# A fused cross-attention and feed-forward kernel: the order of PE's work inside a step

## The chip, the cores and the metric

The kernel runs on one core of one Trainium2 chip. The metric is the device time of the kernel in microseconds (us). A core has five engines with instruction queues of their own: TensorE (PE, the matrix products), VectorE (DVE), ScalarE (ACT), GpSimd (POOL) and SyncE (SP, which here only issues DMAs). Each engine works through its own list of instructions in the order in which it was written, and an instruction that waits for a semaphore keeps those behind it waiting too.

## The reference

One layer of a gated cross-attention block, for 32 batches of 100 rows of x (256 wide) and 1444 context positions each.

```
q = LN(x) Wq^T + bq;  k = ctx Wk^T + bk;  v = ctx Wv^T + bv        # 16 heads of 16
probs = softmax(mask(clip(q k^T / 4, -50, 50)))                   # 100 x 1444 for each head
delta = residual_scale * ((probs v) Wo^T + bo)
x = x + tanh(g_xattn) * (LN(delta) * gamma + beta)
h = silu(bitlinear(LN(x), w1)) * bitlinear(LN(x), w2)              # 704 wide, quantised
out = x + tanh(g_ffn) * bitlinear(h, w3)
```

## The kernel before

**Tiles.** The context of a batch is cut into 12 tiles of 121 positions (the last has 113), and into 3 chunks of 4 tiles. The 12 tiles are 12 *steps* of a batch; 32 batches make 384 steps. Everything is a software pipeline written out by hand: for each engine there is a function `batch` that says what the engine does in step n, and semaphores tie the engines together. There is no planner.

**A step on PE** (`batch` at L1436) is made of these blocks:

- `scores(b, n, 0)` and `scores(b, n, 1)` (L1291, matmuls at L1303): each half is four matmuls, eight head pairs in two halves. Half k of step n writes one of two PSUM buffers `sc`; the halves alternate, so half 0 always uses `sc0` and half 1 always `sc1`. A half must wait until ACT has read the half of the same number of the step before: `pe.wait_ge(exp_done, SCORE.after(b, q) - NSC)` with `NSC = 2`. I call the two blocks S0 and S1.
- `context(0)` and `context(1)`: the two halves of one *context item*, which prepares the next chunk. There are 12 items for a batch, of two kinds: a key item (`k_item`, L1344, three matmuls a half) and a value item (`v_item`, L1358, six matmuls a half). Each chunk has items k0, k1, v0, v1, one in a step. The items of a batch run in the steps n = 4 to 11 of the batch before and n = 0 to 3 of its own. A value item waits until DVE has finished the key item of the same bank, two steps before it (`k_lo_done`). I call the blocks C0 and C1.
- The small products, all in the bank `mb`: the transposition of x (`x_turn`, n = 4), the query projection (`x_query`, n = 5), the output projection (`delta`, n = 3), and those of the feed-forward part: `x2_turn` (n = 7), `up` for gate and up columns in two halves (g0 at n = 8, u0 and g1 at n = 9, u1 at n = 10), `h_turn` (n = 1) and `down` (n = 2).
- `attend`, the *value visit*: in the steps n = 1, 5 and 9 PE multiplies four finished tiles of probabilities by their values, 128 matmul instructions (L1323).

The feed-forward part works on groups of 128 rows, of which there are 25 in 3200 rows. So it is not in every batch: 24 batches have a group for `delta`, `x2_turn` and `up` (23 of these among the first 31 batches), 23 batches have one for `h_turn` and `down` (22 among the first 31). x is turned and projected for the next batch in each of the first 31 batches.

**A step on ACT** (`batch` at L686): the copy of the context item that PE did in the step before (L623 for k, L632 for v), then `exps(b, n, 0)`, then the copy of a small product out of `mb` if there is one in this step (hT at L671, xnT at L651, bd at L661, x2T at L666, th and gs at L678 and L679 for a gate product, us at L684), and last `exps(b, n, 1)` (both at L611). I call the two exponentials E0 and E1. E0 reads what S0 wrote, and E1 what S1 wrote.

```
                    exps(b, n, 0)
                    ...
                    if gd and n in (9, 10):
                        ffn_up(gd, n - 9)
                    if gd and n in (8, 9):
                        ffn_gate(gd, n - 8)
                    ...
                    exps(b, n, 1)
```

**A step on DVE** (`batch` at L1045): the second half of a key item (L837), the clip of the tile before (L846, it needs both exponentials of it), and pieces of the two normalisations and quantisations. After the visit of step 1 it reads the finished attention sums (L915 to L926), and only then, in its step 2, comes the key item that v1 of the third chunk needs on PE in step 3.

Of the kernel before, what the change touches and what calls it, by code (L numbers as in the profile page):

```python
# [41 lines left out]
def flamingo_block(nc, x, ctxT, maskT, g_xattn, g_ffn, wqT, bq, wkT, bk, wvT, bv, woT, bo,  # L42
# [66 lines left out]
    with es:  # L109
# [157 lines left out]
        def stacked_count(b, u):  # L267
            own = b.base or isinstance(b.n, int) and b.n == NB - 1
            return 16 * 3 * NQ * (b.n + 1) - (16 * 3 * (NQ - NQ // 2) if own and u == NCH - 1 else 0)

        def full_group(b):

            g = S * (b.row + 1) // P - 1
            if b.row < 0 or g < S * b.row // P:
                return None
            return whole(g, NG if b.base else 0)
# [12 lines left out]
        def st_slot(b, u):  # L289
            return (NCH * b.par + u) % NKS  # L290
# [978 lines left out]
        def _(pe):  # L1269
# [14 lines left out]
            def weight_sums():  # L1284

                pe.wait_ge(s_seta, SETA["abs5"])
                pe.wait_ge(act_x, X_A.after(whole(1), "bd11"))
                T_.matmul(mb[:, 0:6], ones[:, :], wabs[:, :], start=True, stop=True).then_inc(s_sett, 1)

            def scores(b, n, k):  # L1290
                q = n * STEPS + k  # L1291
                if k == 0 and n % TPC == 0:
                    pe.wait_ge(k_stacked[n // TPC], stacked_count(b, n // TPC))
                    if not b.base and b.row == NB - 1 and n // TPC == NCH - 1:
                        pe.wait_ge(k_stacked_last, 16 * 3 * (NQ - NQ // 2))
                    if n == 0:
                        pe.wait_ge(q_stacked[b.par], 16 * 3 * NQ * (b.pair + 1))
                if not (isinstance(b.n, int) and b.n == 0 and q < NSC):
                    pe.wait_ge(exp_done, SCORE.after(b, q) - NSC)
                t0 = (n % TPC) * TT  # L1300
                for e in range(SPB):
                    pr = SPB * k + e
                    last = T_.matmul(sc[q % NSC][0:TL[n], e // 2, (e % 2) * PW:(e % 2 + 1) * PW],  # L1303
                                     k_st[st_slot(b, n // TPC)][:, pr % NQ, pr // NQ, t0:t0 + TL[n]],
                                     q_st[b.par][:, pr % NQ, pr // NQ, :], start=True, stop=True)
                last.then_inc(sc_ready, 1)

            def pv(b, n, half, first_batch=False):
                if half == 0:
                    pe.wait_ge(clip_done, TILE.after(b, n))  # L1310
                    if n % 2 == 0:
                        pe.wait_ge(v_done, VE.after(b, f"{n // TPC}{(n % TPC) // 2}"))
                        if b.base:
                            pe.wait_ge(care_v, GUARD_V.after_row(b, f"{n + 1}1less"))
                    if n == 0 and not first_batch:
                        pe.wait_ge(dve_att, A_V.after(b.plus(-1), "z1"))
                e = e_sb[e_slot(b, n)]
                for a in range(2):
                    for j in range(NQ):
                        pr = half * NQ + j  # L1320
                        col = half * PW + a * S

                        last = T_.matmul(pvb[QR * j:QR * (j + 1), col:col + S],  # L1323
                                         v_sb[0:TL[n], n, pr, 2 * a:2 * a + 2, :].rearrange("p x d -> p (x d)"),
                                         e[0:TL[n], pr * PW + a * S:pr * PW + (a + 1) * S],
                                         start=(n == 0 and half == 0 and a == 0), stop=(n == NT - 1),
                                         skip_group_check=True)
                if half == 1:
                    last.then_inc(pv_done, 1)
# [33 lines left out]
            def ctx_item(b, w, half):  # L1363
                u, r = divmod(w, 4)
                if r < 2:
                    k_item(b, u, r, half)
                else:
                    v_item(b, u, r - 2, half)

            def x_turn(b, user, older):  # L1370
                pe.wait_ge(dve_x, X_V.after(b, "xn"))
                if user:
                    pe.wait_ge(dve_post, D_V.after(user, "dl"))
                elif older:
                    pe.wait_ge(result_done, older.n + 1)
                elif not b.base and b.row == 2:
                    pe.wait_ge(s_setv, SETV["mean"])
                for k in range(KT):
                    last = T_.transpose(mb[:, k * S:(k + 1) * S], xn[:, k * P:(k + 1) * P], identf[0:S, 0:S])
                last.then_inc(pe_x, 1)  # L1380

            def x_query(b):
                pe.wait_ge(act_x, X_A.after(b, "xnT"))
                for o in range(KT):
                    for k in range(KT):
                        last = T_.matmul(mb[:, o * S:(o + 1) * S], wq[:, k, o * P:(o + 1) * P], xnT[:, k, :],  # L1386
                                         start=k == 0, stop=k == KT - 1)
                last.then_inc(pe_x, 1)
# [10 lines left out]
            def x2_turn(b):  # L1399
                pe.wait_ge(dve_post, D_V.after(b, "x2q"))  # L1400
                for k in range(KT):
                    last = T_.transpose(mb16[:, k * P:(k + 1) * P], x2q[:, k * P:(k + 1) * P], identb[:, :])
                last.then_inc(pe_post, 1)
# [24 lines left out]
            def down(b):  # L1428
                pe.wait_ge(act_post, D_A.after(b, "hT"))
                if not b.base and b.row == 0:  # L1430
                    pe.wait_ge(s_setv, SETV["w3c"])
                for k in range(FT):
                    last = T_.matmul(mb[:, 0:H], hT[:, k, :], w3q[:, k, :], start=k == 0, stop=k == FT - 1)  # L1433
                last.then_inc(pe_post, 1)

            def batch(b, own, nxt, prev):  # L1436
                c, d = b.plus(1), b.plus(-1)
                gd, ge = full_group(d), full_group(b.plus(-2))
                first = not prev
                for n in range(NT):  # L1440
                    group = [(b, i) if i >= 0 else (d, i + NT) for i in range(n - LAG - VISIT + 1, n - LAG + 1)]
                    has_pv = n % VISIT == 1 and (n > VISIT or prev)

                    def context(half):

                        if n >= ITEM and nxt:
                            ctx_item(c, n - ITEM, half)
                        if n < ITEM and own:
                            ctx_item(b, n - ITEM + NT, half)

                    def attend():

                        if has_pv:
                            for pb, pn in group:
                                pv(pb, pn, 0, first)
                                pv(pb, pn, 1, first)

                    scores(b, n, 0)
                    context(0)
                    if not b.base and b.row == 1 and n == 2:  # L1460
                        weight_sums()
                    if ge and n == 2:
                        down(ge)
                    if nxt:
                        if n == 4:
                            x_turn(c, gd, ge)
                        if n == 5:
                            x_query(c)
                    if gd:
                        if n == 3:  # L1470
                            delta(gd, d)
                        if n == 7:
                            if nxt:
                                pe.wait_ge(act_x, X_A.after(c, "bd11"))
                            x2_turn(gd)
                        if n == 8:
                            up(gd, 0, 0)
                        if n in (9, 10):
                            up(gd, n - 9, 1)
                    attend()  # L1480
                    if not nxt and n == NT - 1:
                        for pn in range(NT - VISIT, NT - LAG):
                            pv(b, pn, 0)
                            pv(b, pn, 1)
                    if ge and n == 1:
                        h_turn(ge)
                    if gd and n == 9:
                        up(gd, 1, 0)
                    scores(b, n, 1)
                    context(1)  # L1490


            def keep_warm(bank, count):
# [92 lines left out]
```

## Time and profile before

| | |
|---|---|
| median of 3 runs | 1322.6 us (1320.51 to 1323.1) |
| the profiled execution, its own time | 1319.38 us |
| its span, first to last instruction | 1317.6 us |
| busy PE, DVE, ACT, POOL | 1295.8, 1082.4, 947.3, 364.8 us |
| mean granted TensorE clock | 0.996 of full speed |

The profile's engines run in parallel, so the busy times don't add up. A group of instructions on PE shows the time of each matmul from its start to its modelled end; since matmuls are pipelined, these overlap, and the time that a block of matmuls really takes from PE is read from the chain of waits, where each piece ends as the next begins. PEld is the weight load of a matmul.

### The profile page before, as it was taken

The page shows a single profiled execution, that of the slowest core. Times are in us where ns is not written, and L with a number is a line of the kernel's source. Part 1 is how long each engine was busy: PE and PEld are TensorE (multiplying, and loading weights), DVE is VectorE, ACT ScalarE, POOL GpSimd, SP SyncE. Part 2 cuts the span into 40 slices and gives each one's busy share as a digit, 9 for nine tenths or more (in the row PEclk, how much of TensorE's full clock was granted, in tenths as well). Part 3 has the DMA queues.
Part 4 walks back from the last instruction along what each step waited for, and adds up shares of the span by engine and source line. Part 5 has one row for each costly group of instructions (what it writes and reads, how often), then busy time and mean ns, then how long its engine had stood idle before and what let it go on. Part 6 is the DMA issues. An engine that isn't in the chain of part 4 may idle for free.

```text
span 1317.6 us, 47530 instructions
## 1 busy us (share of the span) xinstructions
PE 1295.8 (98%) x19956; PEld 1192.8 (91%) x19956; DVE 1082.4 (82%) x2167; ACT 947.3 (72%) x1561; POOL 364.8 (28%) x594
## 2 busy tenths in 40 slices
PE   9999999999999999999999999999999999999996
PEld 8999999999989999999999999999999999999985
DVE  5688888789888789886889886889878889878875
ACT  3877777767777767777767777767777767777771
POOL 3221233231233231322331322331223331223320
PEclk9999999999999999999999999999999999999998
DMA  7977767776767766768766777776777676777540
GB/s 205 259 170 169 178 157 190 191 169 168 176 154 195 182 166 168 176 165 198 177 171 166 170 172 194 181 170 163 181 176 189 171 171 165 171 178 192 141 98 11
DMA packets 121420, 225.39 MB, mean 171 GB/s; under 512 B 29674, under 2 KB 89870, under 8 KB 121198
## 3 DMA queue, kind: packets, MB, share of 16 engines
q1 hardware_dynamic: 106968, 200.58, 62.6%
q0 software_dynamic: 12576, 20.42, 6.3%
q8 instruction: 159, 2.61, 0.9%
q10 hardware_dynamic: 1654, 1.27, 0.4%
q14 instruction: 63, 0.52, 0.1%
HBM read 57.27 MB, written 3.28 MB: 46 GB/s over the span
## 4 chain that ended last, share of the span: by engine, by line
PE 86%; DVE 5%; issue 2%; SPq 2%; DMA 1%; POOL 1%; ACT 1%; ACTq 0%; DVEq 0%; POOLq 0%
PE sc L1303 22%; PE pvb L1323 19%; PE cb L1358 18%; PE cb L1344 18%; PE mb L1418 2%; SPq L337 2%; PE mb L1386 2%; PE mb L1396 2%; DMA k_st<-k_lo 1%; PE mb L1433 1%; PE cb L1496 1%; DVE zt L926 1%; PE mb L1425 1%; DVE e_sb L846 1%; DVE k_lo L837 1%
## 5 line engine op out<-in xcount | busy, mean ns | idle before, releaser
L611 ACT ACTIVATE e_sb<-sc 121x800 f32<-121x800 f32 (+1 forms) x768 | 645.3, 845 | 178.4 <-PE sc L1303 166.8
L1303 PE MATMUL sc<-q_st,k_st 96*121 96x200 f32 (+1 forms) x3072 | 467.4, 274 | 4.3 <-DMA k_st<-k_lo 2.3
L1303 PEld LDWEIGHTS sc<-q_st,k_st 96*121 96x121 f32 (+1 forms) x3072 | 409.8, 184 | 34.9 <-issue 7.7
L846 DVE TENSOR_SCALAR e_sb<-e_sb,hi_b 121x1600 f32<-121x1600 f32 (+1 forms) x384 | 410.9, 1072 | 19.5 <-ACT e_sb L611 19.3
L1323 PE MATMUL pvb<-e_sb,v_sb 121*32 121x100 f32 x12288 | 285.0, 250 | 1.2 <-DVE e_sb L846 1.2
L1323 PEld LDWEIGHTS pvb<-e_sb,v_sb 121*32 121x32 f32 x12288 | 263.3, 110 | 24.6 <-issue 19.5
L837 DVE SCALAR_TENSOR_TENSOR k_lo<-cb,bk_c,k_hi 128x484 fp32r<-128x484 f32 (+1 forms) x192 | 134.5, 700 | 125.6 <-ACT k_hi L623 125.4
L1358 PE MATMUL cb<-wv_hi,c_hi 128*121 128x256 f32 (+1 forms) x768 | 221.9, 289 | 1.3 <-DVE k_lo L837 0.4
L498 POOL DMA_DIRECT2D q_st<-bd_hi x256 | 147.1, 578 | 263.7 <-DVE bd_lo L894 258.0
L1358 PE MATMUL cb<-wv_hi,c_lo 128*121 128x256 f32 (+1 forms) x768 | 216.2, 282 | 0.0
L1358 PE MATMUL cb<-wv_lo,c_hi 128*121 128x256 f32 (+1 forms) x768 | 215.8, 281 | 0.0
L1344 PE MATMUL cb<-c_hi,wk_hi 128*128 128x484 f32 (+1 forms) x384 | 153.9, 401 | 1.3 <-ACT v_sb L632 1.3
L1344 PE MATMUL cb<-c_hi,wk_lo 128*128 128x484 f32 (+1 forms) x384 | 145.9, 380 | 0.0
L1344 PE MATMUL cb<-c_lo,wk_hi 128*128 128x484 f32 (+1 forms) x384 | 145.8, 380 | 0.0
L1358 PEld LDWEIGHTS cb<-wv_hi,c_hi 128*121 128x121 f32 (+1 forms) x768 | 141.6, 184 | 3.5 <-DVE k_lo L837 3.3
L1358 PEld LDWEIGHTS cb<-wv_hi,c_lo 128*121 128x121 f32 (+1 forms) x768 | 140.7, 183 | 0.1
L1358 PEld LDWEIGHTS cb<-wv_lo,c_hi 128*121 128x121 f32 (+1 forms) x768 | 140.1, 182 | 0.0
L623 ACT ACTIVATE k_hi<-cb,bk_c 128x484 fp32r<-128x484 f32 (+1 forms) x192 | 127.0, 662 | 2.0 <-PE cb L1344 1.9
L477 POOL TENSOR_TENSOR d_r<-d_ve,minus_half 128x1 f32<-128x1 f32 x25 | 31.4, 1258 | 345.3 <-DVE d_ve L956 345.3
L813 DVE TENSOR_TENSOR c_lo<-c_in,c_hi 128x968 fp32r<-128x968 f32 (+1 forms) x96 | 113.3, 1180 | 0.0
L632 ACT ACTIVATE v_sb<-cb 121x512 f32<-121x512 f32 x160 | 96.2, 602 | 9.8 <-PE cb L1358 9.8
L1344 PEld LDWEIGHTS cb<-c_hi,wk_lo 128*128 128x128 f32 x384 | 72.0, 188 | 12.1
(163 smaller groups left out, 1378.4 us busy)
## 6 DMA issues: line engine op xcount, KB each, us to landing
k_st<-k_hi SPq DMA_DIRECT2D x508, 121.0 KB, 3.0
c_in<-in_ctxT SPq DMA_DIRECT2D x64, 484.0 KB, 3.9
k_st<-k_lo SPq DMA_DIRECT2D x254, 121.0 KB, 3.0
k_st<-k_hi SPq DMA_DIRECT2D x252, 119.0 KB, 3.3
c_in<-in_ctxT SPq DMA_DIRECT2D x32, 476.0 KB, 3.9
k_st<-k_lo SPq DMA_DIRECT2D x126, 119.0 KB, 3.0
q_st<-bd_hi POOLq DMA_DIRECT2D x256, 50.0 KB, 3.5
q_st<-bd_lo POOLq DMA_DIRECT2D x128, 50.0 KB, 3.5
```

What stands on the lines that cost most here:

```text
L477: nc.gpsimd.tensor_tensor(d_r[:, :], d_ve[:, :], minus_half[:, :], ALU.pow).then_inc(pool_post, 1)
L498: nc.gpsimd.dma_start(q_st[b.par][QR * part:QR * (part + 1), j, :, :].bitcast(f32), src[QR * j:QR * (j + 1), :, :, :].rearrange("p k a s - ...
L611: nc.scalar.activation(e_sb[e_slot(b, n)][0:TL[n], k * SW:(k + 1) * SW].rearrange("p (o c) -> p o c", o=2), sc[q % NSC][0:TL[n], :, 0:2 * PW],
L623: nc.scalar.activation(k_hi[slot][:, o, 0:CL[u]], cb[o][:, 0:CL[u]], ACT.Identity, bias=bk_c[:, o:o + 1]).then_inc(k_hi_done, 1)
L632: nc.scalar.activation(v_sb[0:TL[n], n:n + 2, :, 0:4:3, :].rearrange("p n q a d -> p (n q) a d"), cb[i][0:TL[n], :].rearrange("p (q a d) - ...
L813: V.tensor_tensor(c_lo[slot][:, :, 0:w], c_in[slot][:, :, 0:w], c_hi[slot][:, :, 0:w].bitcast(f32), ALU.subtract).then_inc(split_done, 1)
L837: V.scalar_tensor_tensor(k_lo[slot][:, o, 0:w], cb[o][:, 0:w], bk_c[:, o:o + 1], k_hi[slot][:, o, 0:w].bitcast(f32), ALU.add, ALU.subtract ...
L846: V.tensor_scalar(e, e, E_LO, hi_b[b.par][0:TL[n], n:n + 1], ALU.max, ALU.min).then_inc(clip_done, 1)
L1303: last = T_.matmul(sc[q % NSC][0:TL[n], e // 2, (e % 2) * PW:(e % 2 + 1) * PW], k_st[st_slot(b, n // TPC)][:, pr % NQ, pr // NQ, t0:t0 + T ...
L1323: last = T_.matmul(pvb[QR * j:QR * (j + 1), col:col + S], v_sb[0:TL[n], n, pr, 2 * a:2 * a + 2, :].rearrange("p x d -> p (x d)"), e[0:TL[n ...
L1344: last = T_.matmul(cb[o][:, 0:w], wt[:, k, o * P:(o + 1) * P], ct[slot][:, k, 0:w], start=i == 0, stop=i == 5)
L1358: last = T_.matmul(cb[i][0:TL[n], half * H:(half + 1) * H], ct[slot][:, k, t0:t0 + TL[n]], wt[:, k, :], start=(k == 0 and a == 0), stop=(k ...
```

## The change

On PE, and on no other engine, the blocks of a step are put in another order. Before: S0, C0, the small products, the visit, the late small products (`h_turn` in step 1 and g1 in step 9, both after the visit), S1, C1. After: S0, S1, C0, C1, the small products, the visit, the late small products. No instruction is added or removed, and the waits are the same ones, each with its block.

```diff
@@ -1456,7 +1456,9 @@
                                 pv(pb, pn, 1, first)
 
                     scores(b, n, 0)
+                    scores(b, n, 1)
                     context(0)
+                    context(1)
                     if not b.base and b.row == 1 and n == 2:
                         weight_sums()
                     if ge and n == 2:
@@ -1486,8 +1488,6 @@
                         h_turn(ge)
                     if gd and n == 9:
                         up(gd, 1, 0)
-                    scores(b, n, 1)
-                    context(1)
 
 
             def keep_warm(bank, count):
```

## Rows read from the trace of the kernel before

**Rows 1.** Busy time of PE: us, share, instructions.

```profile
PE 1295.8 (98%) x19956; PEld 1192.8 (91%) x19956; DVE 1082.4 (82%) x2167; ACT 947.3 (72%) x1561; POOL 364.8 (28%) x594
```

**Rows 2.** Waits: engine, tile, line <- releaser: us, times, longest.

```profile
ACT e_sb L611 <- PE sc L1303: 166.8, 150, 3.1
...
PE sc L1303 <- ACT e_sb L611: 1.6, 4, 0.6
```

**Rows 3.** Windows: busy us by engine (x), then PEclk, DMA.

```profile
500.00:540.00 40.00, 40.00 (x625) 36.86 (x624) 35.12 (x73) 29.91 (x51) 12.44 (x19) 1.00 0.72 175
...
1273.50:1277.00 3.50, 2.78 (x32) 2.11 (x36) 2.63 (x4) 3.37 (x7) 0.26 (x1) 1.00 0.00 0
...
1287.00:1290.00 3.00, 1.40 (x38) 1.01 (x38) 2.90 (x10) 0.78 (x1) 0.00 (x0) 0.89 0.02 5
```

**Rows 4.** Chain of waits, a batch from 502: start, us, what.

```profile
505.60 0.44 PE mb L1425 x6
...
506.50 0.68 PE cb L1344 x3
...
507.59 0.72 PE cb L1358 x6
...
514.52 0.43 PE sc L1303 x4
...
525.28 0.46 PE sc L1303 x4
...
527.87 0.41 PE sc L1303 x4
```

**Rows 5.** Timeline of ACT, same batch: start, us, instruction [idle before].

```profile
506.08 0.81 ACT L671 ACTIVATE hT<-mb 128x768 bf16<-128x768 bf16 x1 [2.97 <-PE mb L1425]
506.79 0.83 ACT L611 ACTIVATE e_sb<-sc 121x800 f32<-121x800 f32 x1
...
514.56 0.35 ACT L651 ACTIVATE xnT<-mb 128x200 f32<-128x200 f32 x1
514.99 0.84 ACT L611 ACTIVATE e_sb<-sc 121x800 f32<-121x800 f32 x1
515.72 0.66 ACT L623 ACTIVATE k_hi<-cb,bk_c 128x484 fp32r<-128x484 f32 x1
516.27 0.84 ACT L611 ACTIVATE e_sb<-sc 121x800 f32<-121x800 f32 x1
...
525.31 0.38 ACT L666 ACTIVATE x2T<-mb 128x256 bf16<-128x256 bf16 x1
525.77 0.84 ACT L611 ACTIVATE e_sb<-sc 121x800 f32<-121x800 f32 x1
...
527.90 0.56 ACT L678 ACTIVATE th<-mb,tiny 128x352 f32<-128x352 f32 x1
...
528.70 0.84 ACT L611 ACTIVATE e_sb<-sc 121x800 f32<-121x800 f32 x1
...
536.46 0.58 ACT L684 ACTIVATE us<-mb,tiny 128x352 f32<-128x352 f32 x1
536.90 0.87 ACT L611 ACTIVATE e_sb<-sc 121x800 f32<-121x800 f32 x1
```

**Rows 6.** Timeline of ACT, then of PE, in the last batch.

```profile
1273.60 1.81 ACT L611 ACTIVATE e_sb<-sc 121x800 f32<-121x800 f32 x2
...
1266.07 0.67 PE L1303 MATMUL sc<-q_st,k_st 96*121 96x200 f32 x4 [0.61 <-ACT e_sb L611]
1266.67 2.96 PE L1323 MATMUL pvb<-e_sb,v_sb 121*32 121x100 f32 x128
...
1275.46 0.67 PE L1303 MATMUL sc<-q_st,k_st 96*121 96x200 f32 x4 [0.20 <-ACT e_sb L611]
```

**Rows 7.** Chain of waits, a batch without a down product.

```profile
620.79 2.93 PE pvb L1323 x128
...
627.76 0.98 PE cb L1358 x6
```

## The prediction

> **What bounds the kernel now.** I read the busy times first: PE works 98% of the span, with DVE at 82% and ACT at 72% [rows 1]. A busy share can hide waits, so I looked at the windows next: from 500 to 540 us, about one batch, PE is busy for all of the 40 us at the full granted clock [rows 3]. The table of waits says the same from the other side: ACT waits 166.8 us in total for the scores, but PE waits for an exponential only 4 times, 1.6 us in all [rows 2]. The chain of waits runs through PE alone for whole batches. So each us of new waiting on PE is a us of the kernel, and a us taken from ACT or DVE is worth nothing.
>
> **The lengths of the pieces.** From the chain [rows 4], in one batch: a score block takes 0.41 us from PE (0.43 behind `x_turn`, 0.46 behind `x2_turn` or `h_turn`), half a key item 0.68, half a value item 0.72. From ACT's timeline, start to start [rows 5]: a copy of a key item holds ACT 0.55 us (515.72 to 516.27), an exponential 0.73 (514.99 to 515.72) before the next instruction starts, and 0.84 until its result is there. The copies of small products ahead of E1 hold it for: hT 0.71 (506.08 to 506.79), xnT 0.43 (514.56 to 514.99), x2T 0.46 (525.31 to 525.77), th and gs together 0.80 (527.90 to 528.70), us 0.44 (536.46 to 536.90).
>
> **The handovers.** PE to ACT: `h_turn` ends in the chain at 505.60 + 0.44 = 506.04 [rows 4], and hT starts at 506.08 [rows 5], so 0.04. ACT to PE: in the last batch a pair of exponentials ends at 1273.60 + 1.81 = 1275.41, and the score block that waited for it starts at 1275.46, so 0.05 [rows 6]. A score block that starts from a wait is longer: 1266.07 to the next piece at 1266.67 is 0.60 against 0.41, since its weights aren't loaded ahead [rows 6]. That is 0.19 more.
>
> **Part 1: S0 and S1 in a row, in a step without a small product.** S1 of the next step needs E1 of this one. Take the tighter kind, the key step, from the start of S0. ACT copies the item of the step before at 0.04, starts E0 at 0.59 and E1 at 1.32 (S1 was ready at 0.82), and its result is there at 2.16, so PE may start at 2.21. PE itself arrives at the next S1 after 0.82 + 1.36 + 0.41 = 2.59. 0.38 us is left: no wait. S0 has more, as E0 is done at 1.43. The matmuls are the same ones. Whether eight score matmuls in a row run at 0.41 for four isn't in the middle batches; at worst the second four lose what the first four lose behind a transposition (0.05, from 0.46 against 0.41), 384 x 0.05 = 19 us, and at best the joined halves of an item save some of their first-matmul delay, a few us. I take nothing, the value nearest to a block that follows another full block.
>
> **Part 2: the small products now come after C1, and E1 waits behind them.** This is the edit's price. ACT's own order has not changed: E0, then the copy of the small product, then E1. Before, S1 and C1 lay behind the small product on PE, so E1 had two blocks, then S0 and C0 of the next step, before PE asked for it. Now the small product (or the visit) is the last thing of the step, and PE asks for E1 right after one score block. Let the small product end at m. ACT starts the copy at m + 0.04, E1 at m + 0.04 + d, and PE may start S1 at m + 0.04 + d + 0.84 + 0.05 = m + 0.93 + d. PE is there at m + 0.41 to 0.46. Stall, with the 0.19 for a block from a wait:
> - xnT (n = 4): 0.93 + 0.43 - 0.43 + 0.19 = 1.12, in 31 batches: 34.7 us.
> - x2T (n = 7): 0.93 + 0.46 - 0.46 + 0.19 = 1.12, in 23: 25.8.
> - g0 (n = 8) and g1 (n = 9, behind the visit): 0.93 + 0.80 - 0.41 + 0.19 = 1.51, 46 times: 69.5.
> - u1 (n = 10): 0.93 + 0.44 - 0.41 + 0.19 = 1.15, in 23: 26.5.
> - hT (n = 1, behind the visit): 0.93 + 0.71 - 0.46 + 0.19 = 1.37, in 22: 30.1.
> Sum 186.6 us. Not in it: `x_query` (n = 5) and u0 (n = 9) stand ahead of a visit, whose 2.93 us [rows 7] cover the copies and E1; `delta` and `down` are read by DVE, not ahead of E1. After each stall ACT has only a context copy and E0 before the next small product or E1, and S0 of that step was issued ahead of the stall, so nothing carries over. Behind the waiting S1 stand C0, C1 and the small product of the next step; the queue of each engine only shifts by the stall.
>
> **Part 3: the visit as the last block.** Its tiles need `clip_done` of the tile two steps back; PE now asks later within the step, so this gets slacker. What gets tighter is what DVE does after the visit of step 1. In a batch without a down product, the visit ends at 620.79 + 2.93 = 623.72 and the value item v1 of step 3 starts at 627.76, 4.04 us later, behind DVE's reading of the sums and its key half; its first half takes 0.98 instead of 0.72 [rows 7]. Before, PE had 0.60 + 0.68 + 0.41 + 0.72 + 0.41 + 0.72 + 0.41 = 3.95 us of work between, so it paid 0.09 + 0.26 = 0.35. Now only S0, S1, C0, C1 of step 2 and S0, S1 of step 3 lie between: 0.60 + 0.41 + 1.44 + 0.82 = 3.27. It pays 0.77 + 0.26 = 1.03, 0.68 more, in 8 batches: 5.4 us. In the others `h_turn` (0.44), its stall and `down` fill this gap; if they did not, 22 x 0.68 = 15 us more.
>
> **Part 4: the rest.** In the last batch there are no context items from step 4 on, ACT is nearly the bound and the same stalls cost little more; on the other hand the last S1 now comes ahead of two tiles of values, which advances the last exponential. I put both together at 0, between -3 and +5. SP's and POOL's transfers wait for S1 of a chunk's last tile, which comes up to one item earlier; the few us that scores wait for them may go: -3.
>
> **The sum.** 186.6 + 5.4 - 3 = 189 us on the profiled execution's own 1319.4 us (span 1317.6 and 1.8 around it) gives 1508. The median of the runs is 3 us above that execution, so I say 1511.
>
> **The rivals.**
> - *The clock falls* (2.4 to 1.2 GHz). The short waits would come often from step 7 to 10: some 5 us in 17. For: after 1287 to 1290, where PE was busy 1.40 of 3.00 us, the granted clock is down to 0.89 in that stretch. Against: from 1273.5 to 1277 it was busy 2.78 of 3.50 in small pieces and kept the full clock [rows 3]. My stalls are all below 1.6 us with 2 us and more of matmuls between. If some 3 us of matmuls ran at half clock once in 23 batches: 23 x 3 = 70 us, about 1580. The Trainium skill ("TensorE: Matmul & The Clock Gate", section "A second HAM failure mode: psum-queue depth-cycling") tells of a kernel whose frequent micro-idles between groups of matmuls made the clock fall again and again; by that rule it would go this way. The rows at 80% busy speak against it here.
> - *ACT becomes the bound in plain steps too.* The 0.38 us of Part 1 is the only reserve. If an exponential or a handover is that much slower when S0 and S1 come together, each of the some 230 plain steps loses perhaps 0.2: 46 us, 1557.
> - *The stalls are partly hidden*: if the weights of a waiting S1 are loaded ahead, the 0.19 goes 145 times, 28 us: 1483.
> - *Faster.* S0 and S1 in a row give ACT its second half sooner, items in one piece run closer, and value items get two more blocks ahead of them. This wins if E1 is not behind the small product, that is, if ACT did E1 first. Its price is bounded by what PE has to give: the few us of waits for DMA, DVE and ACT and a few for joined halves, at most 12: 1310. ACT's order is in the code and in its timeline (hT, then E at 506.79) [rows 5], so it needs the stalls of Part 2 to be wrong altogether.
> - *No change*: the same, with the gain also zero: 1322.
>
> **How the numbers follow.** My forecast (stalls of Part 2 as counted, 1490 to 1535) 0.68; hidden in part (1460 to 1490) 0.10; ACT-bound 0.08; clock 0.06; something of the stalls only half there (1350 to 1460) 0.03; no change 0.02; faster 0.03. The range from 1465 to 1550 holds the forecast, the hidden case and the lower half of ACT-bound, and takes in the bounds of Parts 1 and 3. A measurement of this kernel tells changes of about 0.2% (2.6 us) from none. Slower by more than that 0.95, within it 0.02, faster 0.03.
>
> **What would show it.** PE's waits for ACT's exponentials go from 1.6 us to about 160 us, some 145 times, the longest 1.3; they stand in steps 1, 4, 7, 8, 9 and 10 ahead of S1 of the next step, and in no other. In the chain, a copy (hT, xnT, x2T, th and gs, us) and an exponential stand between two PE pieces. PE's busy share falls to about 89% (159 of the 187 us are idle, 28 are longer blocks). ACT's wait for scores shrinks, its wait for `mb` grows. If PE waits in the plain steps, the second rival holds; if PEclk drops below 1.00 in the middle, the first. A time below 1450 would mean that E1 was not held by the copies, and the step that failed would be Part 2.

## The result, and the profile after

| | before | after |
|---|---|---|
| median | 1322.8 us (1320.51 to 1323.1, 4 runs) | 1508.4 us (1507.95 to 1512.39, 4 runs) |
| profiled execution, its own time | 1319.38 | 1507.95 |
| its span | 1317.6 | 1506.2 |
| busy PE, DVE, ACT | 1295.8, 1082.4, 947.3 | 1329.8, 1079.0, 961.4 |
| mean granted clock | 0.996 | 0.993 |

The changed kernel takes 1.1422 times as long (95% interval 1.1405 to 1.1438). The profiled executions differ by 188.6 us; the forecast was 189. The forecast for the profiled execution was 1508, and for the median 1511.

The page of the changed kernel has this line of busy times, to be held against [rows 1]; then come lines of its table of waits, for [rows 2] (engine, tile, line <- releaser: us in total, times, longest).

```profile
PE 1329.8 (88%) x19956; PEld 1204.3 (80%) x19956; DVE 1079.0 (72%) x2167; ACT 961.4 (64%) x1561; POOL 349.1 (23%) x594
```

```profile
PE sc L1303 <- ACT e_sb L611: 154.4, 153, 1.3
...
ACT e_sb L611 <- PE sc L1303: 95.3, 95, 2.8
...
PE cb L1358 <- DVE k_lo L837: 6.4, 9, 0.8
...
PE sc L1303 <- DMA k_st<-k_lo: 0.3, 1, 0.3
```

PE waited for exponentials 4 times for 1.6 us before, and does it 153 times for 154.4 us now, never longer than 1.3 us. Seven of the 153 waits stand in the last batch. Of the 188.6 us, PE is idle in 154.6, and busy for the other 34.0 (1329.8 - 1295.8), because blocks that start from a wait are longer; the forecast had 159 and 28. ACT's own wait for scores fell from 166.8 to 95.3 us: it gets them sooner, and that is worth nothing.

The chain of waits of the changed kernel, one full batch, with the pieces of PE that enclose each stall (start us, us, what). It answers to [rows 4].

```profile
567.06 2.91 PE pvb L1323 x128
569.96 0.46 PE mb L1425 x6
...
572.71 1.42 PE cb L1358 x12
...
580.10 0.19 PE mb L1379 x2
...
582.10 1.34 PE cb L1344 x6
...
591.94 0.14 PE mb L1402 x2
...
593.94 1.33 PE cb L1344 x6
595.26 0.33 PE mb L1418 x2
...
597.98 1.33 PE cb L1344 x6
...
602.52 0.42 PE mb L1418 x2
602.93 0.02 issue
602.96 0.03 ACT th L678
602.98 0.07 issue
603.05 0.02 ACTq L610
603.07 0.34 issue
603.41 0.46 ACT gs L679
603.87 0.74 ACT e_sb L611
604.60 0.04 issue
604.65 0.67 PE sc L1303 x4
605.32 1.42 PE cb L1358 x12
606.74 0.33 PE mb L1418 x2
...
609.08 1.43 PE cb L1358 x12
...
614.79 2.90 PE pvb L1323 x128
```

In the middle one stall stands in full: g1 ends at 602.93, ACT copies it (th, gs), then does E1 from 603.75, and at 604.65 PE can start S1. Between 602.93 and 604.65 PE has had nothing but S0. From visit to visit the batch takes 614.79 - 567.06 = 47.73 us. ACT's timeline of that batch shows what holds E1 in the other steps; it answers to [rows 5].

```profile
580.31 0.34 ACT L651 ACTIVATE xnT<-mb 128x200 f32<-128x200 f32 x1 [1.10 <-PE mb L1379]
580.54 0.83 ACT L611 ACTIVATE e_sb<-sc 121x800 f32<-121x800 f32 x1
...
592.10 0.38 ACT L666 ACTIVATE x2T<-mb 128x256 bf16<-128x256 bf16 x1 [1.07 <-PE mb L1402]
592.38 0.83 ACT L611 ACTIVATE e_sb<-sc 121x800 f32<-121x800 f32 x1
```

### The profile page after: what moved, and what is told of

It is laid out like the page before. It is cut to its first block, busy times and chain, and to the rows that moved or that the text cites. A ratio compares the mean times of both kernels' runs of the same rounds, so it can differ in the third digit from the quotient of the medians.

```text
span 1506.2 us, 47530 instructions
## 1 busy us (share of the span) xinstructions
PE 1329.8 (88%) x19956; PEld 1204.3 (80%) x19956; DVE 1079.0 (72%) x2167; ACT 961.4 (64%) x1561; POOL 349.1 (23%) x594
## 4 chain that ended last, share of the span: by engine, by line
PE 77%; ACT 10%; issue 7%; DVE 4%; POOL 1%; SPq 1%; DMA 1%; ACTq 0%; DVEq 0%; POOLq 0%
PE sc L1303 18%; PE pvb L1323 17%; PE cb L1358 17%; PE cb L1344 16%; ACT e_sb L611 8%; PE mb L1418 2%; PE mb L1386 2%; ACT gs L679 1%; PE mb L1396 1%; PE mb L1433 1%; DVE zt L926 1%; PE mb L1425 1%; SPq L337 1%; DMA c_in<-in_ctxT 0%; DVE k_lo L837 0%
## 5 line engine op out<-in xcount | busy, mean ns | idle before, releaser
L611 ACT ACTIVATE e_sb<-sc 121x800 f32<-121x800 f32 (+1 forms) x768 | 623.2, 842 | 95.4 <-PE sc L1303 95.3
L1303 PE MATMUL sc<-q_st,k_st 96*121 96x200 f32 (+1 forms) x3072 | 447.4, 280 | 154.9 <-ACT e_sb L611 154.4
L1303 PEld LDWEIGHTS sc<-q_st,k_st 96*121 96x121 f32 (+1 forms) x3072 | 375.9, 185 | 197.4 <-ACT e_sb L611 181.6
L846 DVE TENSOR_SCALAR e_sb<-e_sb,hi_b 121x1600 f32<-121x1600 f32 (+1 forms) x384 | 404.2, 1055 | 68.6 <-ACT e_sb L611 66.9
L1344 PE MATMUL cb<-c_hi,wk_hi 128*128 128x484 f32 (+1 forms) x384 | 149.6, 390 | 0.8 <-DVE c_hi L807 0.8
L678 ACT ACTIVATE th<-mb,tiny 128x352 f32<-128x352 f32 x48 | 26.6, 554 | 96.1 <-PE mb L1418 96.1
```

The lines of the kernel that those rows point to most:

```text
L611: nc.scalar.activation(e_sb[e_slot(b, n)][0:TL[n], k * SW:(k + 1) * SW].rearrange("p (o c) -> p o c", o=2), sc[q % NSC][0:TL[n], :, 0:2 * PW],
L846: V.tensor_scalar(e, e, E_LO, hi_b[b.par][0:TL[n], n:n + 1], ALU.max, ALU.min).then_inc(clip_done, 1)
L1344: last = T_.matmul(cb[o][:, 0:w], wt[:, k, o * P:(o + 1) * P], ct[slot][:, k, 0:w], start=i == 0, stop=i == 5)
```

## The experiments

All times are medians, and each ratio is to the kernel before, measured beside them on the same chip. Its own median was 1321.1 us beside experiments 1 to 4, 1321.3 beside 5 and 6, and 1322.5 beside 7. An edit is shown against the changed kernel unless the text says otherwise. A *full batch* here has both `h_turn` and `down` and the products of `x2_turn` and `up`, and is measured from the visit of its step 1 to the next such visit.

**1. E1 ahead of the copies, on ACT alone.**

```diff
                     exps(b, n, 0)
+                    exps(b, n, 1)
                     if ge and n == 1:
                         h_turned(ge)
...
-                    exps(b, n, 1)
```

> PE's new order is kept; on ACT the second exponential E1 of a step now runs right behind E0, ahead of the copy of the small product. Theory (the loss is the wait of S1 for an E1 that stands behind the copy of a small product that PE finished one score block earlier): all 145 stalls go, 184 us of the 189; the value item behind the attention sums keeps its 5 us and the DMA waits stay gone, so 1322 to 1327 us, and PE's wait for E1 is back at a few us. Rival 1 (eight score matmuls in a row, or items done in one piece, cost PE time by themselves): the time stays above 1480. Rival 2 (the visit at the end of the step holds DVE up): most of the loss stays too, 1450 or more.

Measured: 1338.1 us, ratio to before 1.0127 (1.0103 to 1.0151). With PE's new order untouched, 170 of the 186 us go (against the changed kernel's own median). This shows the cause, and throws out rivals 1 and 2. But it misses its own range by 11 us. A full batch takes 40.51 us in it against 40.06 before, and its chain shows where (this kernel's chain, steps 9 to 11):

```profile
542.47 0.42 PE mb L1418 x2
...
543.36 0.46 ACT gs L679
543.82 0.55 ACT k_hi L623
544.38 1.46 ACT e_sb L611 x2
545.84 0.04 issue
545.88 0.65 PE sc L1303 x4
```

Now th, gs and the key copy stand ahead of *both* exponentials of step 10, and S1 of step 11 waits for the second one. That is 0.45 us in the 23 batches with gate products, 10 us; the value item behind the sums keeps its 5. The waits for the DMA of k_st are not gone either, though I had expected that: they are 3.1 us in this run's table.

**2. Only the gate copies go behind E1.**

```diff
+                    exps(b, n, 1)
                     if gd and n in (8, 9):
                         ffn_gate(gd, n - 8)
...
-                    exps(b, n, 1)
```

> As the changed kernel, but ACT's copies of the gate products alone (th and gs, steps 8 and 9) go behind E1; the copies of xT, hT, x2T and the up product stay ahead of it. Theory: each stall stands for itself, so 46 x 1.57 = 72 us go and the other 99 stay: 1436 us, and the waits of PE for E1 lose 46 x 1.31 = 60 us, down to about 94. Rival (the stalls are one shared backlog of ACT, that moves to the next product when one is taken away): less than 30 us is won, 1480 or more.

Measured: 1435.3 us (1.0862, 1.0829 to 1.0894). PE's waits for exponentials:

```profile
PE sc L1303 <- ACT e_sb L611: 91.8, 106, 1.2
```

A hit in the time (1436 was forecast) and in the wait (91.8 against 94): the stalls of different products add up, each for itself.

**3. C1 put back to the end of the step, S1 stays early.**

```diff
                     context(0)
-                    context(1)
...
                     if gd and n == 9:
                         up(gd, 1, 0)
+                    context(1)
```

> As the changed kernel, but the second half of the context item is put back to the end of the step: S0, S1, C0, small products, visit, late ones, C1. ACT's order stays. Theory: C1 (0.68 us for a key item, 0.72 for a value item) now lies between the small product and the next S1 and is taken off every idle time, and a block that still starts from a wait costs 0.26 more: xT 0.05+0.26, x2T about 0 to 0.1, gates 0.63+0.26, up 0.21+0.26, hT 0.50+0.26; times 31, 23, 46, 23, 22 this is 81 us; the value item after the sums is as before. So 1319 + 81 - 3 + 3 = 1400 us. Rival 1 (the pair S0 S1 costs by itself): little won, above 1480. Rival 2 (all or nothing: any cover hides it all): 1325.

Measured: 1406.1 us from two runs (1403.2 and 1409.1), ratio 1.064 (1.0603 to 1.0678), 6 above the forecast.

```profile
PE sc L1303 <- ACT e_sb L611: 52.9, 99, 1.3
```

Half a context item as cover takes 101 of the 154 us of waiting away. This is the dose to which a wait of fixed length should answer; neither "the pair costs" nor "all or nothing" would give it. The 6 us were not taken apart.

**4. The whole context item at the end.** S0, S1, small products, visit, late ones, C0, C1.

```diff
                     scores(b, n, 1)
-                    context(0)
-                    context(1)
...
                     if gd and n == 9:
                         up(gd, 1, 0)
+                    context(0)
+                    context(1)
```

> S0, S1, small products, visit, late ones, and then the whole context item C0, C1. ACT's order stays. Theory: 1.36 us or more of item and 0.41 of S0 lie between a small product and the next S1, against 0.93 plus the copy's 0.23 to 0.80, so no stall is left, and the value item behind the sums has 1.3 us more ahead of it than in the changed kernel, so its wait goes too (8 x 0.35 us less than before). 1316 to 1321 us, the same as before or up to 0.4% faster. Rival 1 (the pair S0 S1 or the undivided item costs PE by itself): above 1480 in the full form, or 1330 to 1345 if eight score matmuls in a row run at the weight loads' pace. Rival 2 (the late order delays the small chain on DVE): 1330 or more, with waits of PE for DVE.

Measured: 1342.3 us (1.0155, 1.0131 to 1.0178): the 145 stalls are gone, yet the time is 21 us above the range's upper end. Two causes are in its trace. From visit to visit a full batch takes 552.63 - 512.01 = 40.62 us, 0.56 more than before, since ACT comes late by 0.1 to 0.3 in the steps 2, 9 and 10: 13 us in the 23 batches with gate products. The other one I had not looked for: PE stops in the middle of a visit and waits for nothing that the profile shows (timeline of PE, then two windows with busy times and, third from the end, the granted clock).

```profile
260.77 0.88 PE L1323 MATMUL pvb<-e_sb,v_sb 121*32 121x100 f32 x11 [2.31 <-issue]
```

```profile
258.00:261.00 3.00, 0.69 (x29) 0.47 (x19) 1.08 (x4) 0.00 (x0) 2.65 (x5) 0.97 0.98 242
261.00:264.00 3.00, 3.00 (x17) 2.35 (x10) 0.00 (x0) 0.00 (x0) 0.00 (x0) 0.50 0.92 199
```

There are 8 such stops, 9.5 us together, and behind the long one shown the clock is at 0.50 of full speed, the lower of its two levels (1.2 GHz), for a whole context item. That item takes 2.70 us in the chain instead of 1.34, and behind each of the three long stops some 1.5 us are lost in this way. With it the two causes make 27 of the 27.3 us by which the profiled executions differ (1346.69 against 1319.38).

**5. Experiments 4 and 1 together.**

> The last two together: PE does S0, S1, small products, visit, late ones, C0, C1, and ACT does E1 right behind E0. In the run with the context last, PE's pieces of a full batch sum to 40.6 us against 40.06 before: two stretches where ACT, which still has E1 behind the copies, comes late by 0.1 to 0.3. In the run with E1 first, th, gs and the key copy of step 9 stand ahead of both exponentials of step 10. Theory (ACT's order against PE's is all of it): with both, neither is left, a full batch is back at 40.0 to 40.1, and the wait for the value item behind the sums stays gone: 1316 to 1324 us, plus up to 12 us if PE runs into the same unexplained stops in the middle of a visit that the context-last run has (three of 2.2 to 2.6 us with the clock falling behind them). Rival (pairs and undivided items cost PE by themselves 0.5 us a batch): a full batch stays at 40.5 or more, 1335 to 1345.

Measured: 1325.6 us (12 runs, 1319.1 to 1331.3), ratio 1.0019 (1.0003 to 1.0034), no better than before. Its visits in the chain:

```profile
507.89 2.89 PE pvb L1323 x128
...
547.82 2.89 PE pvb L1323 x128
```

A full batch is 39.93 us, less than the 40.06 of before. So pairs of score blocks and undivided items cost PE nothing; the rival falls. What is left are 9 stops inside visits, 10.3 us, as in experiment 4. They may be why the twelve runs lie so far apart, but only one of them was profiled. 23 x 0.13 = 3 us is the most that this order would win without them; that is worked out, not measured.

**6. The key half ahead of the sums.** In the 8 batches without `h_turn` and `down` DVE reads the attention sums in step 2, behind the key half, instead of in step 1.

```diff
                         if n == 2:
+                            if not ge:
+                                attention_read(d)
+                                sums_inverse(d)
                             attention_out(d)
...
-                        if n == 1:
+                        if n == 1 and ge:
                             attention_read(d)
                             sums_inverse(d)
```

> As the changed kernel, but in the 8 batches without h_turn and down products DVE does the key half of step 2 ahead of reading the attention sums instead of behind it. Theory: the value item of step 3 waited for it (PE's waits for DVE 6.4 us and 9 blocks from a wait with 0.26 more), so about 8 x 1.03 = 8 us go: 1500 us. Rival (the wait is for something else, for instance for ACT's copy): 1506 to 1510, and the wait stays.

Measured: 1500.7 us (1500.0 to 1501.4), against 1508.4 of the changed kernel, which was measured on another occasion. The kernel before was 1.5 us faster beside this experiment, and the two profiled executions differ by 6.6 us (1507.95 and 1501.36), so 6 to 8 us is what the edit won. The wait of value items for DVE has left the table. The changed kernel's chain at such a batch, which answers to [rows 7]:

```profile
702.76 2.94 PE pvb L1323 x128
...
709.75 1.67 PE cb L1358 x12
```

The visit ends at 705.70 and the value item starts 4.05 us later, as in [rows 7]; its twelve matmuls take 1.67 instead of 1.44. The 4.04 us are DVE's, the same in both kernels to 0.01, and only the work that PE has in between changed.

**7. The other half of the change alone.** On the kernel before, C1 goes forward behind C0, and S1 stays last.

```diff
                     context(0)
+                    context(1)
...
                     scores(b, n, 1)
-                    context(1)
```

> The other half of the change alone, on the kernel before: C1 is moved forward behind C0, S1 stays at the end of the step (S0, C0, C1, small products, visit, late ones, S1). ACT's order stays. Theory: the small product and the visit lie ahead of the step's own S1, so E1 isn't asked for until S0, C0, C1 and more of the next step are done, and no stall of the 145 is there; in a plain key step ACT's round from one S1 to the next S0 is 0.04 + 0.73 + 0.55 + 0.84 + 0.05 = 2.21 us against 2.16 of PE, but those steps lie beside visits or products that give it time. The value item behind the attention sums has the same 3.27 us ahead of it as in the changed kernel, so the 5 us of Part 3 come in full: 1323 to 1330 us. With the run that put C1 last this makes the two halves of the change unequal and not additive. Rival 1 (an undivided item costs PE by itself, or both halves of the change bear on the loss alike): 1350 to 1430. Rival 2 (ACT's 0.05 us too much in plain key steps bites, with 0.26 for each block from a wait): 1340.

Measured: 1353.2 us (1.0238, 1.0217 to 1.0259): a miss, worse than my range and than the rival with 1340. None of the long stalls is there, as the theory had it, but a full batch takes 556.56 - 515.71 = 40.85 us. The chain and ACT's timeline at step 10:

```profile
549.54 0.41 PE sc L1303 x4
549.95 0.02 issue
549.97 0.64 PE sc L1303 x4
```

```profile
547.45 0.46 ACT L679 ACTIVATE gs<-mb 128x352 f32<-128x352 f32 x1
547.80 0.85 ACT L611 ACTIVATE e_sb<-sc 121x800 f32<-121x800 f32 x1
548.52 0.68 ACT L623 ACTIVATE k_hi<-cb,bk_c 128x484 fp32r<-128x484 f32 x1
549.06 0.86 ACT L611 ACTIVATE e_sb<-sc 121x800 f32<-121x800 f32 x1
```

I had counted ACT's round for a plain step only. With gs ahead of it, E1 of step 9 starts at 547.80, the key copy and E0 of step 10 follow without a gap, and E0 ends at 549.92; PE wants S0 of step 11 at 549.95. PE waits for 0.02 us and pays 0.25, because the block from a wait takes 0.64 instead of 0.39. In five places of a batch together such delays make 0.8 us, some 18 us in the 23 batches with gate products, and the value item of Part 3 about 5. The batches without `x2_turn` and `up` lose as well: from the visit of step 1 to the next they take 39.2 us instead of 37.9, and 7 of them make 9 us: four times in such a batch a pair of score blocks takes 1.01 to 1.05 us instead of 0.83. That would fit the round that my second rival had named, ACT's 2.21 us against PE's 2.16, but what each of them waits for was not taken apart. Together this is 32 of the 33.0 us between the profiled executions (1352.41 and 1319.38).

Side by side: before 1322, C1 forward alone +31, S1 forward alone (experiment 3) +85, both +186. The halves don't add (31 + 85 = 116), since what counts is the cover that is left between a product and the next S1: with either half undone there is still something in it.

## Why the prediction was right

**The bound.** PE had no spare time, so its new waits came through in full (154.6 us of idle time and 34.0 of longer blocks make the whole difference); DVE and ACT got slacker, and it was worth nothing.

**Part 1, the pair.** The plain steps run as counted: two steps in a row, 0.84 + 1.31, without a wait at the changed kernel's rate, and experiment 5 shows the pair and the undivided item to be free. But the 0.38 us of reserve is real only where no copy is in ACT's round; experiments 1, 4 and 7 ran into that. In a full batch of the changed kernel it cost nothing, since the terms of Part 2 make up the whole difference; in the last batch PE waits 0.51 us twice in plain steps, and in the kernel before 0.61 and 0.51 us there.

**Part 2, the stalls.** The step is right, and each term can be read from the chain above: from the end of the product to the next context block, less the two score blocks that would be there anyway (0.82; 0.84 behind xT, 0.87 behind hT and x2T).

| product | forecast | measured | times | us |
|---|---|---|---|---|
| xnT | 1.12 | 582.10 - 580.28 - 0.84 = 0.98 | 31 | 30.4 |
| x2T | 1.12 | 593.94 - 592.08 - 0.87 = 0.99 | 23 | 22.8 |
| g0, g1 | 1.51 | 597.98 - 595.59 - 0.82 = 1.57 | 46 | 72.2 |
| u1 | 1.15 | 609.08 - 607.07 - 0.82 = 1.19 | 23 | 27.4 |
| hT | 1.37 | 572.71 - 570.42 - 0.87 = 1.42 | 22 | 31.2 |

That is 184.0 us against 186.6. Two sizes were off, in opposite directions. The copies xnT and x2T hold ACT 0.23 and 0.28 us, not 0.43 and 0.46: in the kernel before they started right behind E0, and here ACT has been idle for 1.1 us before them. And a score block from a wait takes 0.67 us to the next context block, not the 0.60 that I read ahead of a visit [rows 6], so every stall costs 0.07 more. The two errors nearly cancel (10 us less, 10 us more); that the sum hit closer than its terms is luck. For one full batch the terms make 7.72, and the trace has 47.73 - 40.06 = 7.67. The count was one short: the last batch has an `h_turn` in step 1 as well, and its S1 waits 1.17 us, which is 1.4 us more that stands in no part of the forecast.

The rival of the partly hidden stalls had the weights of a waiting S1 loaded ahead of its wait. The timeline of weight loads shows that they are not: behind g1 the engine's loads stand idle until the exponential is done, and start with the block.

```profile
604.64 0.50 PEld L1303 LDWEIGHTS sc<-q_st,k_st 96*121 96x121 f32 x4 [1.49 <-ACT e_sb L611]
```

**Part 3, the value item behind the sums.** Forecast 5.4 us. Measured in one batch 0.77 + 0.23 = 1.00 against 0.35 before, 0.65, so 5.2 in eight. Experiment 6, which takes the wait away, gets 6 to 8 us back of 8 x 1.00.

**Part 4, the rest.** The stretch from the `delta` product of the last batch to the `h_turn` behind that batch takes 1478.53 - 1448.51 = 30.0 us after and 1288.68 - 1262.42 = 26.3 before, 3.8 more, and the end behind it 1.2 less: together 2.5, inside the -3 to +5. Up to that `delta` product the kernels differ by 1448.51 - 1262.42 = 186.1 us, while the terms make 184.0 + 5.2 + 1.4 = 190.6. Of the 4.5 us that are left over, 1.6 are waits for DMA that have gone (forecast 3): up to there they were 1.9 us before and are 0.3 after. The rest was not taken apart. For the whole of the kernel before its table has this line:

```profile
PE sc L1303 <- DMA k_st<-k_lo: 2.3, 4, 1.0
```

**The clock.** It had its rival, and the rival is wrong for the whole of the run but not for the last batch. Windows of the changed kernel, busy us by engine, then the granted clock:

```profile
590.00:610.00 20.00, 15.65 (x221) 13.53 (x221) 11.58 (x22) 12.67 (x22) 8.12 (x14) 1.00 0.58 139
...
1454.00:1457.00 3.00, 2.49 (x67) 2.17 (x56) 1.71 (x4) 1.19 (x2) 2.24 (x4) 1.00 0.77 175
1457.00:1460.00 3.00, 2.30 (x15) 1.71 (x14) 2.86 (x7) 2.57 (x5) 2.16 (x3) 0.76 0.02 8
1460.00:1463.00 3.00, 2.32 (x10) 1.89 (x10) 2.09 (x3) 1.89 (x4) 0.00 (x0) 0.50 0.00 0
```

In the densest stretch of stalls PE is busy 15.65 of 20 us and has the full clock. The Trainium skill ("TensorE: Matmul & The Clock Gate", section "A second HAM failure mode: psum-queue depth-cycling") tells of frequent micro-idles that bring the clock down; some 145 idle times of 0.7 to 1.3 us did not do so here. In the last batch, where there are no context items between the stalls, it did fall to 0.50, the lower level. PE was busy 2.49 of 3.00 us from 1454 at the full clock, and 2.30 of 3.00 us, with 15 matmuls, from 1457, where it fell. Which of these idle times brought it down was not tested. A visit took 4.73 us there instead of 2.90, and two score blocks 1.13 instead of 0.67. So the fall cost some 3 us once, and I had given it no place in Part 4.

## What to carry to other kernels

When two engines hand work back and forth, look for the order of the *other* engine before you move a block: here PE's new order was nearly harmless by itself (16 us of the 186 stayed when ACT's order was changed to fit), and the loss was that ACT still did E1 behind the copy of a product which PE now finished only one score block before it needed E1. The stall is (handover + what stands ahead on the other engine + the result's own time + handover) less the work that your engine has between, and it can be read off the profile before the change is made. Where two engines are near balance, count the round for the worst step with all its extras, not for the plain one; and count for each block that starts from a wait, however short the wait, what its weight loads cost.

## What was not expected

- A block of four score matmuls that starts from a wait of only 0.02 us takes 0.64 us instead of 0.39 (experiment 7). The forecast had such a fixed part of a wait's price, with 0.19 us; it is 0.25, it comes in full with the shortest wait, and the table of waits does not show it.
- PE stops inside visits for 0.4 to 2.6 us for no releaser that the profile shows, in experiments 4 and 5 only, 8 and 9 times (experiment 3 has one such stop, of 0.7 us, in a context item at 62.5 us). In experiment 4 they are at 46.9, 111.0, 260.8, 474.5, 624.6, 838.3, 987.9 and 1201.5 us; from the fourth on, each comes 363.2 to 363.8 us after the last but one. That is nine batches, and every second batch without `h_turn` and `down` is nine batches from the last but one, too. The three long stops (2.2 to 2.6 us, at 260.8, 624.6 and 987.9) fall where the DMA engines are busy 0.91 to 0.96 of the time, from 1 us ahead of the stop to its end; but at two of the short ones the share is 0.25 and 0.26 (111.0 and 838.3), so full DMA engines are not the whole of it. That PE waits there for its own code, delayed by other transfers, would be one reading of the long ones; no run tested it, and it stays open.
